# State products of gated linear attention as one-head 64x64 tiles reading the scan's output

## The reference, cut to what matters

```python
q = (x @ W_q).reshape(Bn, Tn, H, dk)          # H = 16 heads, dk = dv = 64
k = (x @ W_k).reshape(Bn, Tn, H, dk)
v = (x @ W_v).reshape(Bn, Tn, H, dv)
a = jax.nn.sigmoid(x @ W_gate + b_gate).reshape(Bn, Tn, H, dk)
def step(S, qkva):
    q_t, k_t, v_t, a_t = qkva
    S = a_t[..., None] * S + k_t[..., None] * v_t[..., None, :]
    o_t = jnp.einsum('bhk,bhkv->bhv', q_t, S)
    return (S, o_t)
...
x = x + 0.5 * _L0_ffn_ref(_layernorm(x), ...)
x = x + _L0_attn_ref(_layernorm(x), W_q, W_k, W_v, W_gate, b_gate, W_o)
x = x + 0.5 * _L0_ffn_ref(_layernorm(x), ...)
```

## Time and profile before

| | |
|---|---|
| median of 3 runs | 2407.74 us (2407.22 to 2409.39) |
| the profiled execution: its time | 2403.1 us |
| its span, first to last instruction | 2401.4 us |
| granted TensorE clock, mean of the span | 0.925 |
| TensorE matmul busy | 2022.3 us (84%) |
| TensorE weight load busy | 1792.5 us (75%) |
| VectorE busy | 1352.4 us (56%) |
| ScalarE busy | 1186.0 us (49%) |
| state products, line 676: busy, records | 73.4 us, 512 |
| copies into state_in, line 1306: busy, count | 49.4 us, 128 |

### The profile page before, as it was taken

How to read it: one execution, slowest core, us unless ns; L and a number is a source line. 1 busy time by engine, 2 the same in 40 slices (tenths; PEclk the granted TensorE clock), 3 DMA queues, 4 the chain that set the end, 5 groups by cost and what they waited for, 6 DMA issues and landing times.

```text
span 2401.4 us, 37764 instructions
## 1 busy us (share of the span) xinstructions
PE 2022.3 (84%) x13967; PEld 1792.5 (75%) x13968; DVE 1352.4 (56%) x3033; ACT 1186.0 (49%) x1927; POOL 266.6 (11%) x267
## 2 busy tenths in 40 slices
PE   5169999999995988989889898974299999999990
PEld 5158889898984777777777777774298899988890
DVE  6345555555455758576585857655155545555544
ACT  1055566655463646455464554621266556665530
POOL 1720000000002100001010000006400000000226
PEclk6579999999997999999999999985599999999995
DMA  6332221222122000000000000002411221222214
GB/s 257 107 138 80 96 96 44 70 96 96 47 77 65 19 5 14 12 8 19 1 19 5 14 1 2 1 1 79 168 45 71 96 79 44 72 94 96 77 59 140
DMA packets 95405, 150.86 MB, mean 63 GB/s; under 512 B 9583, under 2 KB 76678, under 8 KB 94068
## 3 DMA queue, kind: packets, MB, share of 16 engines
q1 hardware_dynamic: 83008, 116.46, 14.2%
q0 software_dynamic: 12288, 32.91, 4.4%
HBM read 98.84 MB, written 51.15 MB: 62 GB/s over the span
## 4 chain that ended last, share of the span: by engine, by line
PE 65%; DVE 11%; PEld 7%; POOL 6%; issue 5%; ACT 3%; DMA 1%; PEldq 1%; POOLq 0%; DVEq 0%; SPq 0%
PE bank L538 27%; PE bank L557 12%; PE bank L609 8%; PE bank L692 4%; PEld bank L557 4%; POOL expert_in L426 4%; PEld bank L538 3%; PE bank L633 3%; PE bank L676 3%; PE bank L680 3%; POOL halves L433 2%; DVE wide L1302 2%; PE bank L502 2%; DVE temp L1306 2%; DVE halves L1313 1%
## 5 line engine op out<-in xcount | busy, mean ns | idle before, releaser
L538 PE MATMUL bank<-halves 128*128 128x512 f32 (+2 forms) x3744 | 767.9, 365 | 22.4 <-DVE halves L1112 22.4
L538 PEld LDWEIGHTS bank<-halves 128*128 128x128 f32 x3744 | 647.0, 190 | 127.5 <-issue 24.7
L557 PE MATMUL bank<-halves 128*128 128x256 f32 (+1 forms) x3288 | 403.1, 283 | 3.0 <-issue 3.0
L557 PEld LDWEIGHTS bank<-halves 128*128 128x128 f32 (+1 forms) x3288 | 397.3, 189 | 5.7 <-issue 4.8
L794 ACT ACTIVATE temp<-bank,bias_now 128x512 f32<-128x512 f32 (+1 forms) x312 | 200.2, 642 | 365.4 <-PE bank L538 365.1
L1125 DVE SCALAR_TENSOR_TENSOR temp<-bank,bias_fc,temp 128x512 f32<-128x512 f32 (+1 forms) x312 | 216.1, 693 | 224.8 <-ACT temp L794 220.2
L609 PE MATMUL bank<-halves 128*128 128x512 f32 x1152 | 287.3, 401 | 2.0 <-DVE halves L1253 2.0
L1132 DVE TENSOR_TENSOR halves<-temp,halves 128x512 fp32r<-128x512 f32 (+1 forms) x312 | 198.0, 635 | 125.6 <-ACT halves L750 123.1
L609 PEld LDWEIGHTS bank<-halves 128*128 128x128 f32 x1152 | 212.7, 190 | 50.4 <-DVE halves L1253 2.4
L433 POOL DMA_INDIRECT halves<-expert_out,read_slot x96 | 104.6, 1090 | 1192.1 <-DMA expert_out<-rows 648.8
L750 ACT ACTIVATE halves<-temp 128x512 fp32r<-128x512 f32 (+1 forms) x313 | 184.9, 591 | 9.9
(11 more groups left out here) (160 smaller groups left out, 2247.6 us busy)
## 6 DMA issues: line engine op xcount, KB each, us to landing
expert_out<-rows SPq DMA_DIRECT2D x144, 128.0 KB, 1.7
wide<-in_L_ffn_w_c_fc SPq DMA_DIRECT2D x16, 1024.0 KB, 5.4
wide<-in_L_ffn_w_gate SPq DMA_DIRECT2D x16, 1024.0 KB, 7.4
wide<-in_L_ffn_w_c_proj SPq DMA_DIRECT2D x16, 1024.0 KB, 5.5
wide<-expert_in SPq DMA_DIRECT2D x32, 512.0 KB, 4.8
expert_in<-halves SPq DMA_DIRECT2D x9, 1024.0 KB
x<-in_L_attn_x SPq DMA_DIRECT2D x4, 1024.0 KB, 9.6
out_x<-x SPq DMA_DIRECT2D x32, 128.0 KB, 2.3
```

The costliest lines, as they stand in the source:

```text
L538: m = pe.matmul(bank[at + b][:, 0:w], a[:, kc, j * P:(j + 1) * P], v[:, kc, 0:w], start=(i == 0), stop=(i == len(ps) - 1))
L557: mm = pe.matmul(bank[4 + t % 2][0:m, 0:C], a[:, j, o:o + m], v[:, j, :], start=(k == 0), stop=(k == len(ps) - 1))
```

## The change

The tile `state_in`, its clearing and the two copies into it are taken out. For each chunk the state products become two matmuls, one for each head, with 64 rows and 64 columns of the array: head 0 with partitions 0 to 63 on both sides, head 1 with partitions 64 to 127. Their weights are read from `states` itself, where a head's state of one chunk is 64 words that lie six words (24 bytes) apart. Both heads write bank 5, each in its own 64 partitions. Their last matmul raises a new semaphore, `states_used`; the scan of the next pair waits for it, since `states` is now read by TensorE. The scan itself raises `state_ready`, and DVE waits for that ahead of keeping the final state.

```diff
-ATT_CLEARS = 7
+ATT_CLEARS = 6
...
-        state_in = part(temp, 512, SUPER, P)
...
+        states_used = sem("states_used")
...
+                    by_chunk = states.rearrange("p (n c) -> p c n", n=DH)
                     for c in range(SUPER):
-                        pe.matmul(bank[5][:, c * P:(c + 1) * P], state_in[:, c, :], qd[g % 2][:, c, :],
-                                  start=(c == 0), stop=False, skip_group_check=True)
+                        for h in range(2):
+                            hp = slice(h * DH, (h + 1) * DH)
+                            m = pe.matmul(bank[5][hp, c * P:(c + 1) * P], by_chunk[hp, c + 1, :], qd[g % 2][hp, c, :],
+                                          start=(c == 0), stop=False, skip_group_check=True)
+                    m.then_inc(states_used, 1)
...
-                v.memset(state_in, 0.0).then_inc(att_cleared, 1)
...
                     steps.after(v.tensor_copy(kv[:, :, 1], state[:, g, :]))
-                    steps.after(v.tensor_tensor_scan(states, bank[7][:, 0:DH * (SUPER + 2)], factors, 0.0,
-                                                     ALU.add, ALU.mult))
-                    for h in range(2):
-                        hp = slice(h * DH, (h + 1) * DH)
-                        ins = v.tensor_copy(state_in[hp, :, hp].rearrange("p c n -> p n c"), st[hp, :, 1:SUPER + 1])
-                    ins.then_inc(state_ready, 1)
+                    wait_past(dve, states_used, G)
+                    v.tensor_tensor_scan(states, bank[7][:, 0:DH * (SUPER + 2)], factors, 0.0,
+                                         ALU.add, ALU.mult).then_inc(state_ready, 1)
+                    dve.wait_ge(state_ready, G + 1)
                     v.tensor_copy(state[:, g, :], st[:, :, SUPER + 1]).then_inc(state_kept, 1)
                     dve.wait_ge(state_kept, G + 1)
```

## The result

The changed kernel takes 2367.71 us (median of 4 runs, 2365.19 to 2370.87) against 2407.48 us: a ratio of 0.9838 with a 95% interval of 0.982 to 0.9856, some 39 us faster. The forecast was 2376.5 us, in a range of 2363 to 2398. A second session with the same kernel gave 0.9848 (0.9823 to 0.9873), some 37 us.

What follows compares the result with a forecast made beforehand. PE bounds the attention, idling 49.1 us for the copies ahead of the state products. Seven supertiles win 26 us and the last 5.4, sum 31, with products and strided weights at no cost: 2407.7 - 31 = 2376.5 us, range 2363 to 2398.

Steps and rivals of the forecast that it cites:

- The bound and the copies: Attention rounds: PE sets the pace; without the copies state_ready comes 0.81 us earlier in each of 64 rounds, sum 31 us.
- The second loop over ACT's logarithms: Closes over two rounds, sum_logs held by ACT's logarithms: 17.44 us or 8.72 a round, so a plain round wins 0.75 us.
- My list of signs: What would show it right, such as PE's waits from 53 us to some 20 and sum_logs' waits half a microsecond longer.
- rival D: State products' release: the change does nothing because state_ready was not the releaser; 2408 us, 7% together with B half hidden.
- The state products: Sixteen 64x64 records for eight of 128x128 keep a group at 1.06 us: no change, ends -9 and +3 us.
- Rival A: State products: the two heads' row tiles run one after the other, +68 us, 2445 us in all; 7%.
- The strided weights: State products' weight loads, words six apart: no cost taken, by DVE's line 1308; upper bound +55 us.
- rival B: State products' strided weight loads cost double: in the open 2432 us, 6%; half hidden 2404 us, 7% together with rival D.
- the bound's condition: Strided weight loads: the upper bound of 0.86 us a group, +55 us, holds if no load hides behind a matmul.
- The cleared tile: Clearing on DVE, 0.48 us: covered by a 1.25 us wait for gathered rows; without that cover worth 0.5 us once.
- the new waits: The scan's wait for the previous pair's state products and DVE's for state_ready ahead of line 1308: cost nothing.
- Rival C: Attention rounds: the wait only moves, ACT's logarithms or DVE's order gives back half of the gain; 2392 us, 10%.

Runs made afterwards that it cites:

- the two kernels with one part each: Changed kernel with state_ready held until the old copies are done: ratio 1.0013; kernel before with 128x128 products, released by the scan without copies: 2368.58 us, ratio 0.9847.
- the order kernel: Changed kernel with the state products' order turned, four chunks of one head and then four of the other: 2398.03 us in one run.

## Why the prediction was right

**The bound and the copies.** Right in the mechanism, and close in nearly every round. The forecast gains were 0.81, 0.75, 0.75, 0.3, 0.81 and 0.26 us for the rounds up to pairs 2 to 7; measured are 0.81, 0.78, 0.80, 0.31, 0.82 and 0.29. The second loop over ACT's logarithms shows as DVE's wait of 0.98 us at line 1263, and the rows above close it: 918.25 - 915.31 = 2.94 us from the transposes to sum_logs, 922.12 + 1.45 - 918.25 = 5.32 on to the keys at 923.57, 925.83 - 923.57 = 2.26 on to the products, 923.98 - 917.17 = 6.81 from products to transposes, together 17.33 or 8.66 a round, as measured. The forecast was 8.72; it had 5.48 in the place of 5.32. PE's waits ahead of the products fell to 19.7 us, forecast some 20. My list of signs gave the growth of DVE's wait as half a microsecond; it was 0.81. The last supertile gave 5.5 us for 5.4. That state_ready was the releaser (against rival D) and that the copies are all of the gain is shown by the two kernels with one part each.

**The state products.** Forecast no change, between -9 and +3 us; measured +0.045 us a group, 2.9 us, and 2.2 to 3.3 us by the two single parts. The overlap of the two heads was right, and the order kernel shows that it was needed. Rival A did not come: in one bank and in two a group takes 1.10 us. The rule of the Trainium skill (TensorEngine Tiling (Array Packing), Gotcha 1: PSUM Pressure) is not borne out for these two tiles.

**The strided weights.** Here a step was wrong, though it cost little: I took no cost, by the nearest row, a DVE copy with that stride. Weight loads do suffer: 193 ns for 134, as rival B had it (double per column). How fast a DVE copy reads such words says nothing of TensorE's weight loads. What was right was the bound's condition: the loads hide behind matmuls, and only 0.08 us a group come into the open, 5 us. The rule of the Trainium skill on SBUF lines of 16 bytes (Advanced Engine Details and Errata, Memory Cachelines) agrees with the 193 ns of the loads. The 218 ns of the DVE copy show no such penalty, but its partner of 228 ns writes PSUM, so the two rows are no clean comparison.

**The rest.** The cleared tile and the new waits left no trace: DVE's line 1309 follows the scan within 0.03 us, and no row shows DVE waiting for PE at line 1306. The sum was 31 us; the stretch gained 35.8. Missing in it were the 3.2 us of the slower clock, which I had counted nowhere although the attention's mean of 0.99 held a sign of it, and some 1.5 us in the rounds. The last is small because two misses offset each other, which is luck. Without the copies and with the old products the stretch is 39.1 us shorter, 35.9 apart from the clock, so I had underrated the copies by some 5 us, most of it in the rounds up to pairs 7 and 8; and the new products, which I had put at nothing, took 3.3 back. Rival C, half of the gain lost, did not come.

## What to carry to other kernels

Work out a round's loops, with the second-longest among them, before pricing a removed copy: the gains of six rounds came out of them within 0.05 us. Work taken off the waiting path pays only if what is behind it on the same engine doesn't set the next loop; moving the refinement behind the scan of the logarithms gave back to the microsecond what it won, and moving it into the engine's own wait kept it. Where a copy only rearranges an operand, let TensorE read the operand as it lies, but look at both the weight load's duration and the length of the whole group, since only the second is time.

## What the runs showed of the hardware

- A weight load of 64 columns whose words lie 24 bytes apart takes 193 ns, of packed words 134 ns; sixteen of the first kind beside matmuls make a group of 1.10 us, of the second 1.02.
- Two 64x64 tiles on the diagonal of the array overlap while they write the same PSUM bank in different partitions: 1.10 us for sixteen records in turn, 1.63 us for eight of one tile and then eight of the other, and 1.10 us with two banks. Records of one tile start 0.113 us apart in either order.
- A wait of 1.77 us, which comes once in each of the first seven supertiles, was followed by the lower of the two clocks in two of them in the kernel before, and in two again in the kernel with the products alone; each cost 1.6 us. Why the other five kept the higher clock stays open. In the kernels whose longest wait ahead of the products there is 1.4 us or less I saw no such supertile.
